# A four-layer graph-attention kernel: layer 0's receiver rows sent through memory instead of 16 TensorE transposes, and 14 rounding copies a batch on GpSimd

## The reference

```python
h = maximum(layernorm(x), 0); x = x + gat0(h)   # 4 heads of 64, leaky ReLU 0.2, mask adj != 0, elu
h = maximum(layernorm(x), 0); x = x + gat1(h)   # MLP 256->512, attention without mask (fc), MLP 512->256, attention with mask adj > 0
h = maximum(layernorm(x), 0); x = x + gat2(h)   # 1 head, mask adj > 0 or itself, elu
h = maximum(layernorm(x), 0); x = x + gat3(h)   # 1 head, leaky ReLU 0.01, mask adj != 0, relu
# one attention:
Wh = h @ W
e = leaky_relu(s_src(Wh)[:, None] + s_dst(Wh)[None, :])
out = softmax(where(mask, e, -inf)) @ Wh
```

## Time and profile before

| | |
|---|---|
| three runs | 2833.2, 2834.45, 2836.31 us; median 2834.45 |
| the profiled execution | 2838.34 us; span of its instructions 2836.5 us |
| granted TensorE clock | 0.994 of full speed |
| busy: TensorE, weight loads | 2793.0 and 2492.5 us |
| busy: VectorE, ScalarE, GpSimd | 2454.7, 2281.5 and 648.3 us |
| DMA | 41.83 MB, 15 GB/s on average |

### The profile page before, as it was taken

How to read it: one execution, slowest core, us unless ns; L and a number is a source line. 1 busy time by engine, 2 the same in 40 slices (tenths; PEclk the granted TensorE clock), 3 DMA queues, 4 the chain that set the end, 5 groups by cost and what they waited for, 6 DMA issues and landing times.

```text
span 2836.5 us, 63430 instructions
## 1 busy us (share of the span) xinstructions
PE 2793.0 (98%) x23704; PEld 2492.5 (88%) x23704; DVE 2454.7 (87%) x6405; ACT 2281.5 (80%) x6079; POOL 648.3 (23%) x1051
## 2 busy tenths in 40 slices
PE   7999999999999999999999999999999999999996
PEld 7888889888998898898898888889988989888885
DVE  6898888898888988888988888988889888889875
ACT  5788878888878888888888788788788888887785
POOL 4122122221122221122221122221122211222111
PEclk9999999999999999999999999999999999999998
DMA  2000000000000000000000000000000000000000
GB/s 83 9 9 9 16 16 16 16 1 17 16 16 17 16 2 16 16 16 16 8 9 16 16 16 16 1 16 16 16 16 16 2 16 16 16 16 9 2 9 15
DMA packets 16785, 41.83 MB, mean 15 GB/s; under 512 B 5344, under 2 KB 7392, under 8 KB 16480
## 3 DMA queue, kind: packets, MB, share of 16 engines
q1 hardware_dynamic: 16480, 37.77, 3.8%
HBM read 20.99 MB, written 16.78 MB: 13 GB/s over the span
## 4 chain that ended last, share of the span: by engine, by line
PE 92%; DVE 5%; ACT 2%; issue 1%; SPq 0%; DMA 0%; POOL 0%; POOLq 0%; DVEq 0%
PE bank L597 48%; PE bank L695 23%; PE bank L729 8%; PE bank L683 4%; PE bank L647 4%; PE bank L816 1%; PE bank L671 1%; DVE R L920 1%; PE bank L767 1%; DVE Z L1015 1%; PE bank L773 1%; DVE oTlo L1021 0%; DVE R L1006 0%; PE bank L706 0%; DVE hT2lo L878 0%
## 5 line engine op out<-in xcount | busy, mean ns | idle before, releaser
L695 PE MATMUL bank<-hw,R 128*128 128x257 f32 x3072 | 722.0, 383 | 1.4 <-ACT hw L1241 1.2
L695 PEld LDWEIGHTS bank<-hw,R 128*128 128x128 f32 x3072 | 565.4, 191 | 86.9 <-issue 8.3
L1422 POOL TENSOR_TENSOR rs<-ve,mhalf 128x4 f32<-128x4 f32 x128 | 140.6, 1098 | 1830.2 <-DVE ve L863 1746.1
L920 DVE SCALAR_TENSOR_TENSOR R<-bank,E,mask_ne 128x512 f32<-128x512 f32 x640 | 452.3, 743 | 3.0 <-PE bank L683 2.2
L597 PE MATMUL bank<-wfc_hi,oThi 128*128 128x256 f32 (+1 forms) x1024 | 298.8, 292 | 0.0
L597 PE MATMUL bank<-wfc_hi,oTlo 128*128 128x256 f32 (+1 forms) x1024 | 288.5, 282 | 0.0
L597 PE MATMUL bank<-wfc_lo,oThi 128*128 128x256 f32 (+1 forms) x1024 | 288.5, 282 | 0.0
L729 PEld LDWEIGHTS bank<-hw,R 128*64 128x64 f32 x8192 | 251.0, 138 | 32.4 <-issue 29.2
L729 PE MATMUL bank<-hw,R 128*64 128x65 f32 x8192 | 269.0, 224 | 0.1
L1220 ACT ACTIVATE Z<-bank,rs 128x258 f32<-128x258 f32 (+1 forms) x384 | 176.0, 478 | 47.4 <-PE bank L597 46.5
L597 PEld LDWEIGHTS bank<-wfc_hi,oThi 128*128 128x128 f32 x1024 | 194.1, 190 | 1.0
(11 more groups left out here) (293 smaller groups left out, 8415.1 us busy)
## 6 DMA issues: line engine op xcount, KB each, us to landing
x<-in_x_dram SPq DMA_DIRECT2D x32, 512.0 KB, 3.6
out_dram<-x SPq DMA_DIRECT2D x31, 512.0 KB, 2.6
R<-in_adj_dram SPq DMA_DIRECT2D x2, 512.0 KB, 7.6
Z<-in_L_gnn_mlp_w_dram SPq DMA_DIRECT2D x2, 512.0 KB, 5.6
O<-in_L_gnn_W_fc_dram SPq DMA_DIRECT2D x1, 1024.0 KB, 7.1
out_dram<-x SPq DMA_DIRECT2D x4, 128.0 KB, 1.8
R<-in_L_gnn_W_dram SPq DMA_DIRECT2D x1, 256.0 KB, 4.0
R<-in_L_gnn_W_hand_dram SPq DMA_DIRECT2D x1, 256.0 KB, 6.6
```

The lines of the kernel that those rows point to most:

```text
L695: ins = e.matmul(bk[:, 0:257], P[:, j, i * 128:(i + 1) * 128], hw[:, j, 0:257], start=(j == 0), stop=(j == NBLK - 1))
L920: e.scalar_tensor_tensor(P[:, t, :], bank_of(b, "row", p)[:, :], m["E"][:, 1, h, j:j + 1], mask[:, j, :], ALU.max, ALU.mult).then_inc(up(" ...
L1422: e.tensor_tensor(m["rs" + z][:, :], m["ve" + z][:, :], mhalf[:, :], ALU.pow).then_inc(up("rs", b), 1 if l == 1 else 3)
```

## The change

Four things change.

1. In layer 0 of the batches 1 to 31 (`by_dma`; batch 0 keeps the old way) the four rows are made otherwise. `gather` transposes the 16 columns of E at once, one matmul with a 16x128 result. `turned_row` on VectorE copies these 16x128 numbers from PSUM to SBUF. SyncE writes them to a scratch tensor in memory (`rows_dram`, 8 KB), waits for that to land, and issues two reads that spread two heads' rows each over all 128 partitions, 512 KB each, into `hThi` and `hTlo` of the lane (they are free from the projection on). `weigh` then reads its row from SBUF instead of PSUM.
2. The 14 rounding copies (`o1hi`, `Phi`, `o2hi`, `o3hi`) are steps of `pool_batch` on GpSimd, and no longer of `scalar_batch` on ScalarE.
3. SyncE's queue has more steps: for each batch the load of its `x`, the write, the two reads, the store of the result. The load of batch b stands behind the store of batch b-4, whose buffer it takes.
4. All `TURNS` strings are other ones, and `uses` lists one bank of a batch's ring (`rT`) in place of four.

Some setup waits on weights join two semaphores into one.

```diff
+ROW_LAYERS = (0,)
+LATE = 0
+def by_dma(b, l):
+    return l in ROW_LAYERS and 0 < b < B - LATE
...
     "sp": (
-        "00112233445566778899aabbccddeeffgghhiijjkkllmmnntoouppvqqrrsstuv"
+        "111023220433154426553766487759886a997baa8cbb9dccaeddbfeecgffdhggeihhfjiigkjjhlkkimlljnmmkonnlpoomqppnrqqosrrpt"
+        "ssquttrvuusvvtuv"
...
+        row_d = nc.dram_tensor("rows_dram", (LANES, 16, 128), F32, kind="Internal").ap()
+        def staged_row(s, l):
+            return ends[s][0:16, 512:640] if l == 0 else f32(hT[s]["hi"][0:4, 0, 0:128])
+        def rows_of(s, l, h):
+            return f32(hT[s][PARTS2[h // 2]][:, h % 2, :]) if l == 0 else f32(hT[s]["lo"][:, 0, :])
...
+            def gather(l, nh):
+                w.wait_ge(*freed(b, "rT", l))
+                w.wait_ge(*at("E", b, l, 0))
+                e.transpose(bank_of(b, "rT", l)[0:NBLK * nh, 0:128], m["E"][:, 0, 0:nh, :].rearrange("p h n -> p (h n)"),
+                            ident[:, :]).then_inc(up("row", b), nh)
+                yield
...
-            yield from row(0, 0, 0)
+            if by_dma(b, 0):
+                yield from gather(0, 4)
+            else:
+                yield from row(0, 0, 0)
...
+            def turned_row(l, nh):
+                if by_dma(b, l):
+                    w.wait_ge(*at("row", b, {0: 3, 2: 5, 3: 6, 4: 7}[l]))
+                    if l == 0 and b >= LANES:
+                        w.wait_ge(*at("x3", b - LANES, 3, 1))
+                    e.tensor_copy(staged_row(s, l), bank_of(b, "rT", l)[0:NBLK * nh, 0:128]).then_inc(up("sc", b))
+                    yield
...
-                w.wait_ge(*at("row", b, p))
+                if by_dma(b, l):
+                    w.wait_ge(*at_rows(b, l, h))
+                    row = rows_of(s, l, h)
+                else:
+                    w.wait_ge(*at("row", b, p))
+                    row = bank_of(b, "row", p)[:, :]
...
-                    e.scalar_tensor_tensor(P[:, t, :], bank_of(b, "row", p)[:, :], m["E"][:, 1, h, j:j + 1],
+                    e.scalar_tensor_tensor(P[:, t, :], row, m["E"][:, 1, h, j:j + 1],
                                            mask[:, j, :], ALU.max, ALU.mult).then_inc(up("P", b))
...
-                w.wait_ge(*at("m1a", b, fo))
-                e.copy(oT["hi"][:, fo, :], O1[:, fo, :]).then_inc(up("o1hi", b))
...
             yield from power(e, w, b, 1)
+            for j in range(NBLK):
+                w.wait_ge(*at("m1a", b, j))
+                e.tensor_copy(oT["hi"][:, j, :], O1[:, j, :]).then_inc(up("o1hi", b))
+                yield
+            for j in range(NBLK):
+                w.wait_ge(*at("hs2", b, 3))
+                w.wait_ge(*at("P", b, 4, j))
+                e.tensor_copy(oT["hi"][:, j, :], R[s][:, j, :]).then_inc(up("Phi", b))
+                yield
+            for u in range(4):
+                w.wait_ge(*at("o2", b, u))
+                e.tensor_copy(Rr[s][:, u, :], O1[:, (u + 2) % 4, :]).then_inc(up("o2hi", b))
+                yield
+            for fo in range(2):
+                w.wait_ge(*at("m2a", b, fo))
+                e.tensor_copy(hT[s]["hi"][:, fo, :], Z[s][:, fo * 512:(fo + 1) * 512]).then_inc(up("o3hi", b))
+                yield
...
+            for l in ROW_LAYERS:
+                if by_dma(b, l):
+                    nh = 4 if l == 0 else 1
+                    w.wait_ge(*at("sc", b, l, 5))
+                    e.dma_start(row_d[s, 0:NBLK * nh, :], staged_row(s, l)).then_inc(s_kept[s], 16)
+                    yield
+                    w.wait_ge(*at_kept(b, l))
+                    every = row_d[s].rearrange("(h n) q -> h (n q)", n=NBLK)
+                    if l == 0:
+                        e.dma_start(f32(hT[s]["hi"][:, :, :]), every[0:2].partition_broadcast(128)).then_inc(s_rows[s], 16)
+                        e.dma_start(f32(hT[s]["lo"][:, :, :]), every[2:4].partition_broadcast(128)).then_inc(s_kept[s], 16)
```

## The result

The kernel got slower where 2790 us were forecast: 2933.18 us in the median (2932.09 to 2935.43) against 2834.65 in the same measurement, a ratio of 1.0348 with a 95% interval of 1.033 to 1.0366, +98.5 us. The profiled execution took 2932.09 us, its span 2930.3.

A forecast was written before the change was run, and what follows sets the result against it. The prediction took TensorE's issue distances as the bound. From the profiled 2838.3 us, -53 for removed TensorE work and +8 for waits gave 2793.3, 2789.4 on the median's scale: 2790 us, range 2778 to 2803.

The forecast's parts named there:

- The rows' term: On TensorE: 465 fewer transposes at 0.110 us, -51.2 us, and 23 fewer changes of matmul kind, -1.8: -53.0 us.
- TensorE's 43.5 idle us: On TensorE: the 43.5 us without work were said to lie at the run's ends, 14.6 and 22.4 us.
- rows that land late: Rival, weights' rows from memory: a chain of 9.4 us stalls each batch, 2874 us, or 2843 partly absorbed; chance 0.11.
- a second bound: Rival, VectorE: collisions cost whole copies, 8.7 us a batch; half or more of the gain lost, 2803 to 2828; chance 0.20.
- the cover of 6.8 us: On VectorE: work between row copy and first weight, 6.8 us in batch 14, hides the 5.4 us landing; cost 0.
- the price of the collisions: VectorE against GpSimd's 14 copies: 0 to 3.9 us of VectorE a batch, taken as 2.
- The 0.28: On VectorE: most that one collision costs it, from L1049's rise from 0.684 to 0.967 us; GpSimd loses up to 1.04.
- the ninth: From VectorE to TensorE: of VectorE's extra 70 us, a ninth reaches TensorE, taken as +8 us.
- its +8: On TensorE: +8 us of waits brought by a busier VectorE and held copies.
- the first term: On TensorE: what rows through memory save by fewer transposes and changes of matmul kind, -53.0 us.

The follow-up runs named there:

- order_only: `rows_only` with the rows made by transposes again, the order otherwise that of the change: 2972.68 us, 1.0486 of the kernel before.
- rows_only: The changed kernel with the 14 rounding copies back on ScalarE, placed where GpSimd had begun them: 2919.64 us, 1.03 of the kernel before.
- no_read2: `no_read` with GpSimd's 18 column-sum instructions a batch as memsets too: 2800.73 us, 0.9878 of the kernel before.
- micro: A separate seven-stage kernel: 48 VectorE weights and 48 GpSimd copies alone, then VectorE instructions beside copies; weight 0.665 us alone, 1.02 beside copies.
- no_read: The changed kernel with each of GpSimd's 14 rounding copies as a memset of the same target, place and waits: 2846.43 us, 1.0039 of the kernel before.
- casts_only: The kernel before, with its order and transposes, but the 14 rounding copies on GpSimd where ScalarE had begun them: 2910.87 us, 1.0265.
- rows_planned: The whole computation: rows through memory, rounding copies on ScalarE, and an order newly found by replay for that division: 2840.58 us, 1.002 of the kernel before.
- no_read2_no_rows: `no_read2` with the rows by transposes again, the order otherwise that of the change: 2869.10 us, 1.0122 of the kernel before.
- rows_planned2: `rows_planned` with another order, found by a replay that counts the collisions in: 2846.17 us, 1.0032 of the kernel before.

## Why the prediction was wrong

**What held.** L733 has 528 transposes and L719 31 gathers. The rows' term fits by its number, -53.0 us forecast and -53.0 between `order_only` and `rows_only`; that it fits to a tenth is luck, since the same edit is worth 68.4 beside `no_read2`. The write lands in 1.3 us and the reads in 4.0 and 4.9, so that the first weight can begin some 5.3 us after the copy (5.4 forecast, as 1.8 and 3.6: the two errors cancel); in the whole run VectorE waited once for a row, 0.2 us. The copy from PSUM takes 0.27 us (0.25), a rounding copy on GpSimd 0.60 undisturbed and 0.61 to 0.80 in the medians (0.65). The rival with the right sign, rows that land late, had the wrong mechanism. VectorE's share of the middle stretch came out as forecast, 91%, and below the 92% that was to show a second bound. Two readings were off without weight for the sum: of TensorE's 43.5 idle us only 37.0 lie in the two end stretches (14.6 + 22.4), and the cover of 6.8 us adds up records, which overlap on VectorE (the weight at 1340.12 has 0.74 us, and the next instruction begins 0.66 after it), so it was less.

**The step that failed** is the price of the collisions, in two places: how much time they take from VectorE, and above all the share of it that reaches the end.

*"GpSimd loses up to 1.04 us, VectorE up to 0.28 ... I take half, 2 us" a batch.* VectorE lost 2584.8 - 2490.5 = 94.3 us to the copies' reads, 2.9 a batch and inside the bounds of 0 and 3.9, and 2490.5 - 2440.9 = 49.6 to those of the column sums, for which the price had nothing: together 144 us or 4.5 a batch. The 0.28 was read as a property of VectorE. It was one of the partner. The later of two waits until shortly before the end of the earlier, and behind the 0.28 the earlier one was a column sum (the L1049 of 0.967 us began 0.04 us after an L1438 of 0.46). A copy lasts 0.60, and the loss behind it in the timeline above is 1.10 - 0.74 = 0.36 for the weight and 1.09 - 0.68 = 0.41 for L1105, in `micro` 0.35 every time. The timeline showed an L625 that lost and an L1049 that did not, and I made a rule of it, that GpSimd is the one that loses. That reading left out the row before it in the trace of the kernel before:

```profile
779.46 0.68 DVE L1037 SCALAR_TENSOR_TENSOR Z<-Z,O 128x512 f32<-128x512 f32 x1
```

L625 was issued at 779.73, inside L1037, whose tiles are all in SBUF. As a record takes in the wait, the 1.96 us begin with one, and they don't show that L1049 began inside the *work* of L625. In the timeline above either side loses, whichever comes second. And the price counted the copies alone. Which instructions meet which is made by the order, and in the changed kernel VectorE meets the *old* column sums more often as well: 49.6 us of its time against 16.9 before, 45.7 us of the kernel's against 4.9. Groups by line in `no_read` and, under them, in `no_read2`, where the sums read nothing:

```profile
L957 DVE TENSOR_SCALAR A<-Z,T 128x4 f32<-128x4 f32 x128 | 44.0, 344 | 0.0
L955 DVE TENSOR_SCALAR A<-Z,T 128x4 f32<-128x4 f32 x128 | 42.0, 328 | 4.5
```

```profile
L955 DVE TENSOR_SCALAR A<-Z,T 128x4 f32<-128x4 f32 x128 | 33.6, 262 | 4.5
L957 DVE TENSOR_SCALAR A<-Z,T 128x4 f32<-128x4 f32 x128 | 32.2, 252 | 0.0
```

These two small lines, the scores, have records that are 20.2 us longer in all, a part of which overlaps the next instruction. The weights with a row in SBUF, the six groups of L988 from `hT`, have 379.6, 363.3 and 352.4 us in the changed kernel, `no_read` and `no_read2`: 16.3 us lost to the copies and 10.9 to the sums, 27 of 144. So the larger part fell on VectorE's other work with tiles in SBUF, not on the weights that the change moved there.

The Trainium skill's rule (SBUF — State Buffer, section SBUF: two separate sides) was the better reading: whichever starts first has the shared ports for the whole instruction and the other blocks, and a VectorE instruction with two SBUF inputs is affected only against a GpSimd one that reads SBUF. For copies the trace agrees with both halves: 1.02 beside 0.665 us in `micro`, nothing lost with the row in PSUM, and 86.8 us gone once the copies are memsets. It does not hold for every GpSimd instruction, as the weight beside L665 shows. I had set the rule against a single pair of rows.

*"VectorE's extra 2.25 us x 31 = 70 us, of which a ninth reaches TensorE".* The two kinds of reads cost 2933.18 - 2800.73 = 132.4 us, which is 92% of VectorE's 144 and not 11% (GpSimd's own delays are gone with the reads too, and were not told apart). No row stood behind the ninth: it came from VectorE's 87% and TensorE's few waits, as if VectorE's idle time could take up what came in addition. This step turned the sign. The forecast 70 us with 92% of them would have given -53 + 64 = +11 us, the measured 144 with a ninth -53 + 16 = -37. The likely reason, argued and not shown, is that an order written out as turns fixes which instruction follows which on each engine, and that the lost time comes inside chains (weight to attention, copy to low part to MLP). VectorE still idles for 8 us in a stretch of 92, but little of the delay was taken up there. `casts_only` shows the same at the old order, 74.5 us of VectorE's and 75.5 us of time, so it is not the new order's own fault. The share is no constant, though: the column sums took 45.7 of 49.6 us in the changed kernel, 18.5 of 40.3 in `rows_planned` (2483.9 - 2443.6) and 4.9 of 16.9 in the kernel before. The rival "VectorE becomes a second bound" had the mechanism (8.7 us a batch from whole copies) but let it cost the gain at the most; it could not come out above 2834, as the bound was taken as the sum of VectorE's work, 86 us, and not as a chain through both engines.

**The account.** Without the reads of copies and sums the change is worth 2800.73 - 2830.56 = -29.8 us. These reads cost 132.4 in the changed kernel and 4.9 in the one before: -29.8 + 132.4 - 4.9 = +97.7, measured +98.5. The sum has to come out, being made of the same differences; what it shows is the sizes. If the rows are worth -53 (or -68, by `no_read2_no_rows`), the -29.8 leave 23 to 38 us that the new order and the copies' place cost besides, for which the forecast had no term: its +8 was for a busier VectorE and held copies. Which steps of the order these belong to was not taken apart.

**What stays open.** Rows through memory without the copies on GpSimd should by the first term have left a gain of up to 53 us. No order that I ran for it got it: 2840.6 and 2846.2 against 2834.6. 18.5 us of it are the column sums' reads. In `rows_planned` TensorE is busy for only 22.7 us less than in the kernel before, and it idles for 69.7 us where that one has 43.5; its listed waits are short (the longest line has 9.1 us in all, in `rows_planned2`). The replay that found the orders ends 79 us before the second one's span (2850.3), against 37 for the kernel before, so it is no witness for a cause.

## What to carry to other kernels

Before work goes to GpSimd, list what VectorE does meanwhile: a GpSimd copy or sum that reads SBUF and a VectorE instruction with all its tiles in SBUF can run in turn, and then either can lose much of the other's length. A weight with its row in PSUM lost nothing here, one with its row in SBUF did; and a new order makes new pairs of old instructions. And VectorE's share of 87% was no cover in this kernel with its fixed order: of the time that it lost, 29% to all reached the end, depending on the order.

Two experiments told it apart quickly: a memset in place of a copy, which nearly keeps the engine's time (0.525 us for 0.60) and drops its reads, and a control of the same edit in the kernel before.

## What the runs showed of the hardware

- A VectorE instruction of 128x4 with its input in SBUF, 0.22 to 0.23 us undisturbed in the changed kernel (L955, L957), comes only every 0.56 us beside a series of copies (L67 in `micro`, which has no stage of it alone), while the copies keep their 0.558. So a small instruction can lose more than its own length.
- A VectorE instruction with a row in PSUM and a mask in SBUF, two inputs, is untouched: 31.7 us for 48 beside the copies, where 48 alone with the row in SBUF take 31.9.
- GpSimd's L665, a tensor_scalar of 128x256 and 1.16 us, does not hold VectorE for as long as it lasts: the weight at 1340.12 us, with its row in SBUF, begins 0.40 us into it and takes its usual 0.74.
- A memset on GpSimd (0.525 us for 128x512) in place of a rounding copy of the same size (0.60) took 94.3 us off VectorE's busy time. It does not leave everything untouched: in `no_read` the records of L955 and L957 beside two memsets are 0.97 and 0.84 us long, while the weight behind them begins 0.13 us later and takes its usual 0.74:

```profile
451.17 0.98 POOL L1520 MEMSET hT1hi<- 128x512 f32 x2
451.20 0.97 DVE L955 TENSOR_SCALAR A<-Z,T 128x4 f32<-128x4 f32 x1
451.34 0.84 DVE L957 TENSOR_SCALAR A<-Z,T 128x4 f32<-128x4 f32 x1
451.47 0.74 DVE L988 SCALAR_TENSOR_TENSOR R<-hT2lo,E,mask_ne 128x512 f32<-128x512 f32 x1
```
